# Graph layer on one core: dense-list rows picked by bfloat16 one-hots from three bfloat16 pieces, second list ahead of the first one-hots

## The reference

```python
src = node_feature[edge_src]
parts = [relu(node_feature)]
for t in range(3):
    msg = where(edge_type == t, relu(src @ W_e[t].T + b_e[t]), 0)
    parts.append(segment_sum(msg, edge_dst, num_segments=N))
agg = concatenate(parts, axis=1)
updated = where(node_type == t, agg @ W_n[t].T + b_n[t])      # for the node's own t
out = layernorm(x + updated + node_feature)
```

## Time and profile before

| | us |
|---|---|
| median of 3 runs (1103.03 to 1105.92) | 1103.26 |
| the profiled execution | 1098.69 |
| its span | 1096.9 |
| TensorE busy | 777.3 |
| GpSimd busy | 679.3 |
| VectorE busy | 679.6 |
| ScalarE busy | 147.8 |

### The profile page before, as it was taken

One profiled execution on the slowest core, in us unless ns is written; L12 is line 12 of the kernel. 1 busy time (PEld: TensorE's weight loads), 2 busy tenths in 40 slices (PEclk: granted clock), 3 DMA queues, 4 the chain that ended last, 5 costly groups with the idle time before them and its releaser, 6 DMA issues. The chain is left out here.

```text
span 1096.9 us, 13056 instructions
## 1 busy us (share of the span) xinstructions
PE 777.3 (71%) x4200; PEld 612.9 (56%) x4200; DVE 679.6 (62%) x1499; ACT 147.8 (13%) x396; POOL 679.3 (62%) x718
## 2 busy tenths in 40 slices
PE   5681227768778677677777788778777776878866
PEld 3350126657656555566665666666555665666654
DVE  7985584576656566556566566566566564465644
ACT  1471000011011011011001011001001000111101
POOL 7787524466666666666666666666666665666660
PEclk9895566898888999989889988888999987888989
DMA  6675112233223224233223233133133143132320
GB/s 205 186 262 140 41 53 53 69 63 95 70 68 94 65 73 94 62 77 92 60 81 92 56 83 93 51 89 92 50 91 104 45 128 88 50 90 72 86 54 13
DMA packets 65777, 94.03 MB, mean 86 GB/s; under 512 B 16497, under 2 KB 49233, under 8 KB 65711
## 3 DMA queue, kind: packets, MB, share of 16 engines
q0 software_dynamic: 22432, 45.99, 16.7%
q1 hardware_dynamic: 40577, 43.14, 13.0%
q10 hardware_dynamic: 2702, 4.08, 1.3%
HBM read 80.23 MB, written 12.92 MB: 85 GB/s over the span
## 5 line engine op out<-in xcount | busy, mean ns | idle before, releaser
L618 POOL DMA_INDIRECT tab<-message_table,idx_t x630 | 596.0, 946 | 367.1 <-issue 176.5
L1097 DVE TENSOR_TENSOR work<-key_t,ps 128x378 f32<-128x378 f32 (+1 forms) x180 | 109.7, 611 | 299.2 <-remote 211.0
L1496 PE MATMUL ps<-work,tab 128*128 128x126 f32 x1260 | 199.3, 303 | 49.6 <-DVE acc L1106 25.5
L1496 PEld LDWEIGHTS ps<-work,tab 128*128 128x128 f32 x1260 | 183.5, 218 | 63.8 <-issue 31.2
L1526 PE MATMUL ps<-we_t,order_f 128*128 128x128 f32 x540 | 107.9, 350 | 95.7 <-DVE order_f L1185 59.2
L1526 PEld LDWEIGHTS ps<-we_t,order_f 128*128 128x128 f32 x540 | 87.1, 240 | 109.9 <-DVE order_f L1185 66.2
L1575 PE MATMUL ps<-wn_t,stage 128*128 128x384 f32 x294 | 106.3, 499 | 2.2 <-DVE stage L1250 2.2
L614 POOL DMA_INDIRECT xg<-in_x,esrc_t x67 | 77.2, 1153 | 20.5 <-issue 17.7
L1476 PE MATMUL ps<-we_t,xst 128*128 128x384 f32 x142 | 63.8, 577 | 36.5 <-issue 25.3
L1575 PEld LDWEIGHTS ps<-wn_t,stage 128*128 128x128 f32 x294 | 57.3, 197 | 43.4 <-issue 7.3
L1185 DVE TENSOR_TENSOR order_f<-ps,dst_raw 128x768 f32<-128x768 f32 x45 | 43.1, 958 | 53.1 <-remote 26.8
(11 more groups left out here) (229 smaller groups left out, 941.0 us busy)
## 6 DMA issues: line engine op xcount, KB each, us to landing
tab<-message_table,idx_t POOLq DMA_INDIRECT x630
message_table<-tab SPq DMA_DIRECT2D x24, 384.0 KB
dst_raw<-dense_types SPq DMA_DIRECT2D x45, 192.0 KB
wn_raw<-message_table SPq DMA_DIRECT2D x22, 384.0 KB
src_wide<-dense_lists SPq DMA_DIRECT2D x45, 128.0 KB
xg<-in_x SPq DMA_DIRECT2D x11, 256.0 KB
work<-in_x ACTq DMA_DIRECT2D x10, 256.0 KB
out<-xg SPq DMA_DIRECT2D x10, 256.0 KB
```

The costliest lines, as they stand in the source:

```text
L618: pool.indirect_dma_start(msg[:, slot, :], None, table, bass.IndirectOffsetOnAxis(ap=rows, axis=0)).then_inc(signal, 16)
L1097: dve.tensor_tensor(hot[:, first:first + n, :].rearrange("p c (t w) -> p c t w", w=WIN), keys.broadcast_to((P, n, T, WIN)), iota_win.rearr ...
L1496: ins = pe.matmul(sums_bank(nth), msg[:, column, :], hot[:, column, :], start=(c == 0), stop=(c == n - 1))
```

## The change

Four things are done.

1. `dx` is loaded into a free part of `acc`, earlier in SyncE's order: ahead of the two small stores of `bases` and `estats`, not behind the loads of the self rows. It is split into three bfloat16 pieces whose sum is exact: ScalarE copies `dx` to the first piece, VectorE subtracts it from `dx`, ScalarE copies the rest to the second piece, VectorE subtracts that and writes the third, `dx_last`.
2. `donehot` becomes bfloat16 for both sets, in `dense_wide`. `dense_turn` runs 15 bfloat16 matmuls for each set in place of 5 float32 ones.
3. `list_dense(1)` stands ahead of the first one-hots.
4. The memset of `acc` on VectorE is gone. ScalarE zeroes those columns and the place of `dx` (2360 columns) ahead of its own round 0; the memset at VectorE's start begins later in the row.

```diff
+        dx_parts = tab_flat[:, CHUNKS * D:CHUNKS * D + DX].bitcast(BF16).rearrange("p (m k d) -> p m k d", m=2, d=D)
+        dx = acc[:, 1, HALF + R:HALF + R + DX].rearrange("p (k d) -> p k d", d=D)
...
+        donehot = [words(dense_wide, s * SET_NODES // 2, SET_NODES // 2).bitcast(BF16).rearrange(
+            "p (k i e) -> p k i e", k=DT, i=2) for s in range(SETS)]
+        dx_last = words(first_wide, 0, DX // 2).bitcast(BF16).rearrange("p (k d) -> p k d", d=D)
+        dx_part = (dx_last, dx_parts[:, 1, :, :], dx_parts[:, 0, :, :])
...
             sp.wait_ge(bases_set, 1)
+            sp.dma_start(dx, x[N - SETS * SET_NODES:N, :].rearrange("(k p) d -> p k d", p=P)).then_inc(got_dx, 16)
...
             relu_half(NB, 0, 0, 1, stored=NB // 2 * 16)
+            act.wait_ge(got_dx, 16)
+            act.wait_ge(tab_stored[0], (NB // 2 + 1) * 16)
+            for half in range(1, 4):
+                act.wait_ge(tab_stored[half], NB // 2 * 16)
+            act.activation(dx_parts[:, 0, :, :], dx, ACT.Copy).then_inc(dx_first_set, 1)
             setup_copy(IDX_UNIT, len(UNITS))
...
             act.wait_ge(consts_set, 1)
+            act.wait_ge(dx_rest_set, 1)
+            act.activation(dx_parts[:, 1, :, :], dx, ACT.Copy).then_inc(dx_second_set, 1)
+            act.wait_ge(dx_last_set, 1)
+            act.wait_ge(dense_listed, 1)
+            zero_acc(acc[:, 1, HALF:HALF + R + DX], R + DX)
             iteration(0, True, False)
...
             list_dense(0)
+            dve.wait_ge(dx_first_set, 1)
+            dve.tensor_tensor(dx, dx, dx_parts[:, 0, :, :], ALU.subtract).then_inc(dx_rest_set, 1)
+            list_dense(1)
             dve.wait_ge(iota_moved, 1)
             dve.wait_ge(setup_copied, len(UNITS))
             for g in range(NG):
                 one_hot(0, g)
-            list_dense(1)
+            dve.wait_ge(dx_second_set, 1)
+            dve.tensor_tensor(dx_last, dx, dx_parts[:, 1, :, :], ALU.subtract).then_inc(dx_last_set, 1)
             unpack_dense()
-            dve.memset(acc[:, 1, HALF:HALF + 2 * R], 0.0).then_inc(acc_zeroed, 1)
             first_rows()
             list_loops()
...
                 for s in range(SETS):
                     pe.wait_ge(d_onehot, SETS * j + s + 1)
-                    for k in range(DT):
-                        ins = pe.matmul(dxt_ps[:, :, s * DENSE:(s + 1) * DENSE], dx[:, (SETS - 1 - s) * DT + k, :],
-                                        donehot[s][:, k, :, :], start=(k == 0), stop=(k == DT - 1))
+                    for m, part in enumerate(dx_part):
+                        for k in range(DT):
+                            ins = pe.matmul(dxt_ps[:, :, s * DENSE:(s + 1) * DENSE], part[:, (SETS - 1 - s) * DT + k, :],
+                                            donehot[s][:, k, :, :], start=(m == 0 and k == 0),
+                                            stop=(m == PARTS - 1 and k == DT - 1))
                 ins.then_inc(d_turned, 1)
```

More of the change, by code:

```diff
@@ L55 @@
 SET_NODES = DT * P
+DX = SETS * DT * P
+PARTS = 3
 SET_FIRST = tuple(N - (s + 1) * SET_NODES for s in range(SETS))
@@ L278, in build @@
         dtypes = words(dst_wide, 0, 2 * T * P).bitcast(BF16).rearrange("p (a c) -> p a c", a=2)
-        donehot = [words(whole, 0, SET_NODES).rearrange("p (k i e) -> p k i e", k=DT, i=2)
-                   for whole in (first_wide, dense_wide)]
+        donehot = [words(dense_wide, s * SET_NODES // 2, SET_NODES // 2).bitcast(BF16).rearrange(
+            "p (k i e) -> p k i e", k=DT, i=2) for s in range(SETS)]
+        dx_last = words(first_wide, 0, DX // 2).bitcast(BF16).rearrange("p (k d) -> p k d", d=D)
+        dx_part = (dx_last, dx_parts[:, 1, :, :], dx_parts[:, 0, :, :])
         dhot = words(first_wide, SET_NODES, 2 * T * DW).rearrange("p (i c) -> p i c", i=2)
@@ L839, in link @@
                 dve.wait_ge(vec_step, steps[0])
-            dve.memset(acc[:, 1, HALF + 2 * R:NPAD], 0.0).then_inc(acc_zeroed, 1)
+            dve.memset(acc[:, 1, HALF + R + DX:NPAD], 0.0).then_inc(acc_zeroed, 1)
             dve.wait_ge(got_esrc, 32)
```

8 lines of the change are left out of this document (4 added, 4 removed).

## The result

The change makes the kernel slower, where I had forecast faster. The median of four runs is 1128.61 us (1123.67 to 1133.77), against 1104.59 us (1103.03 to 1108.60) for the kernel before, measured beside it. The ratio is 1.022, with a 95% interval from 1.018 to 1.026.

What follows compares the result with a forecast made beforehand. Hand-overs bound the kernel, no engine being full; ahead of the rounds everything waits for VectorE's list work. 12.96 + 2.4 - 1.5 = 13.9 us off 1103.26 gave 1089.4 us, range 1076 to 1104.

Steps and rivals of the forecast that it cites:

- The price of the turn: In the rounds' dense_turn: thirty bfloat16 matmuls take 1.7 to 2.5 us against 2.24 for ten float32; counted as nothing.
- the lower bound: In dense_turn: 0.056 us a bfloat16 matmul, 1.7 us for thirty, 0.55 us less a round.
- The pace of the rounds does not follow PE's matmul time.: In the rounds: six half rounds take 62.10 and 61.90 us at different clocks; PE idles 4.2 us a round.
- rival C: In the set-up: late sums take back 5.4 us, moved keys 2 more; 1095 to 1100 us, chance 0.13.
- The set-up, 13.9 us: Ahead of the rounds: 12.96 + 2.4 - 1.5 = 13.9 us earlier, VectorE's round 0 at about 137.7.
- What hides it is the wait for `key_t`. The path loses 12.96 us.: In the set-up: the second list fits VectorE's 20.14 us of idle time ahead of the first one-hots.
- the list would start to show: In the set-up: the second list is no longer fully hidden if the keys come 5.6 us earlier.
- rival A: At each round's end: bfloat16 turn longer and PE on the path, 0.8 us a round; 1124 us, chance 0.14.
- B: In the rounds: PE on the path and turn 0.55 us shorter; 1065 us, or 1075 in part; chance 0.13.

Runs made afterwards that it cites:

- e3: Changed kernel with the turn run on the first piece alone, ten bfloat16 matmuls in place of thirty: 1089.67 us, ratio 0.988.
- e4: Changed kernel with the turn run on the first two pieces, twenty bfloat16 matmuls in place of thirty: 1100.61 us, ratio 0.996.
- e1: Kernel before with the second list ahead of the first one-hots and acc columns zeroed by ScalarE, float32 turn kept: 1101.23 us, ratio 0.9955.
- e2: Changed kernel with the second list put back behind the first one-hots: 1136.85 us, ratio 1.029.
- e5: Changed kernel with GpSimd's gathers of round 1 held back until VectorE has listed the loops: 1132.32 us, ratio 1.024.

## Why the prediction was wrong

**The price of the turn: "I put nothing for it".** This is the step that failed most: in the 553 gathers of the middle the rounds lost 33.9 us. The turn's size in the array was right (1.67 us, near the 1.7 of the lower bound). The mistake was to price a run of TensorE instructions by their time alone. In the late condition thirty pairs cost what twenty did not. Fewer turns of twenty pairs stop behind a late sum (one in 45, against 11), and the mask waits less: its idle time is 31.0 us with ten (e3), 53.2 with twenty short ones (e4), 53.1 and 79.9 with twenty long ones (before, e1), 143.3 and 146.6 with thirty (changed, e2). POOL's waits for PE's sums and "remote" add up to 190.6 us in the kernel before and to 224.7 in the changed one, 34.1 us more. That the matmuls added to the turn cause it is shown by e2, e3 and e4; that it is their number and nothing else that they bring with them is argued.

**"The pace of the rounds does not follow PE's matmul time."** True as read from the earlier trace rows, and e3 agrees with it (818.7 us for 553 gathers with the shortest turn, 817.9 before). But I took it as proof of slack. A pause of 1.8 us that comes behind the seventh gather whatever PE's clock is fits a POOL that waits for signals that come late, and then anything which moves a signal past the next pause costs more. For that the old turn left room, and the new one did not. The earlier trace rows held the same warning: 5.4 us between the end of PE's sums and POOL's release. I gave it to rival C, at a chance of 0.13 and for the set-up alone.

**The set-up, 13.9 us.** "What hides it is the wait for `key_t`. The path loses 12.96 us." This step failed too. The keys came at 94.62 us and not at 120.11, so nothing hid the list: it stood on the path in full. The order alone was worth 3.5 us in the median (e1). The prediction had said what follows from earlier keys ("the list would start to show") but gave it no chance. The list itself ran from 96.7 to 112.2 us, ahead of the 101.6 to 114.6 that I had put, with 2.5 us of gaps. The pieces cost what I said: 1.49 and 1.48 us for the subtractions (1.5 forecast), hidden copies, 2.17 us for the zeroing (2.1). Behind the one-hots, too, the sum failed: 2.0 us for `unpack_dense` became 16.2 (from 117.39 to 133.61), and the loops' list got about 4 us of gaps. From the one-hots to DVE's round 0 I had 17.4 us (31.3 before, less 13.9); it took 35.6. Before, the list and `unpack_dense` ran while POOL stood still until 130.06 us and beside the seven gathers that followed, and the loops' list mostly behind these. Now `unpack_dense` comes at the end of an unbroken row of gathers that goes from 84.2 to 129.5 us. The work was moved out of a quiet stretch into a busy one. The gain in POOL was 2.1 us in place of 13.9.

**The rivals.** The measured 1128.6 us lies near the 1124 of rival A, but not by its mechanism: a matmul costs 0.056 us at 2.4 GHz, not 0.1; that its number is near is luck. B falls by e3: a turn shorter by 1.7 us would give 74 us in 44 rounds if PE were the path, and e3 is 11.6 us faster than e1. C had the mechanism, signals of PE that arrive after their rows end, at too small a size and in the wrong place. The range ended at 1104 because A was left out of it; A had been priced on time, and a price on the number of instructions was in none of the cases.

**What is shown and what is not.** Shown: the loss goes with the turn, grows with the number of bfloat16 matmuls in it, is not the place or type of their operands nor the clock, and is absent where signals are prompt. Shown too, by the records of the increments: with thirty pairs PE stops inside the turn until the late increment of the sum ahead of it arrives, which with twenty it hardly ever does. But these stops sum up to only about 11 us. Argued: that the rest of the 33.9 comes through the later mask, and that the whole loss goes by the number of matmuls and not their time (by the order of four kernels). Open: the direct test of number against time in the late condition, what makes signals late, and why the same program on the same chip is in one condition or the other. One rival was not looked at: the recording itself. The ten late traces hold 5800 to 7100 records of semaphore updates, the ten prompt ones about 17600, for nearly the same work. Whether records are lost because signals are held up, or signals are held up by the recording, can't be told from runs that all come with a span and a granted clock.

## What to carry to other kernels

When a wait ends well after its producer's row has ended, look for what is common to all such waits before moving work into the gap: the gap may not be there in the next execution, and work that is moved under the gathers beside which signals come late gets gaps of its own. On an engine whose signals come late, do not price work by its microseconds in the array alone: three cheap matmuls for one dear one were shorter and still cost 2.2%. And before a gain is claimed, compare in both conditions: the same change costs 2.2% in one and nothing in the other (1.0003). An independence from one engine's speed, read from two windows, is no proof of slack against another kind of load.

## What the runs showed of the hardware

Signals can reach their waiters many microseconds after their producer's row in stretches in which GpSimd issues indirect gathers (TensorE's 17.2 us in the kernel before, 102.12 to 119.30, and 13.8 in the changed one, 119.98 to 133.74; VectorE's to itself up to 6.6, in e5), and go on being late for about 4 us behind the last gather (126.4 to 130.47 in e5). Not every signal beside a gather is late: the seven gathers from 130.06 us on in the kernel before left the second list without gaps, the long row of them ahead of 129.5 us in the changed kernel did not.

This is a condition of the execution and not of the program: the kernel before took 1104 us in three series and 921 to 923 in four others, and one chip showed both. GpSimd issues its gathers back to back in the prompt condition too, so gathers alone do not make signals late. In the prompt condition GpSimd's gathers, 1.249 us each, are the whole pace, and 20 small matmuls a turn, a wider turn or the change itself cost at most 0.3%.

TensorE without a semaphore to wait for can fall from one matmul in 0.056 us to one in 0.7 us (838.58 to 840.59 us of the changed kernel), until the increment of a sum ahead of it is delivered (840.61). The Trainium skill ("TensorE: Matmul & The Clock Gate", Back-to-back issue gap) speaks of a 64-deep reorder window through which weight loads and matmuls pass; 26 pairs are 52 instructions. That would fit a window that an undelivered signal keeps from moving on. That the stops end with the delivery is shown (11 of 11 turns, within 0.12 us); that they begin where such a window is full was not tested, and they begin 20 to 29 pairs behind.
